# Local attention: scores of two heads in two 64-row halves of the TensorE array, and the value projection moved

## What is computed

```python
q, k, v = split(shift_token(x) @ wqkv, 3)        # 8 heads x 64
q = l2norm(q) * qs;  k = l2norm(k) * ksc
q, k = rotary_xpos(q, k)                         # a rotation by cos and sin tables
sim = einsum('bhwid,bhwjd->bhwij', bq, bk)       # 128 queries x (previous + own 128 keys)
attn = softmax(where(mask, -max, sim))
x = x + einsum('bhwij,bhwjd->bhwid', attn, bv) @ wo
```

## Time and profile before

| what | us |
|---|---|
| median of three runs (4228.1 to 4229.81) | 4228.54 |
| the profiled execution | 4233.28 |
| its span, first to last instruction | 4231.3 |
| one local attention, from its first to its last instruction (four in a launch) | about 287 |
| one window in its steady part | 17.00 |

### The profile page before, as it was taken

The page is one execution under the profiler, slowest core; times in us unless marked ns, Lnnn a source line. Parts: engine busy times, 40 slices in busy tenths (PEclk is TensorE's granted clock), DMA queues, the critical chain, the costliest instruction groups (busy, mean ns, idle before and its releaser), DMA issues. The chain is left out here.

```text
span 4231.3 us, 60343 instructions
## 1 busy us (share of the span) xinstructions
PE 3778.0 (89%) x19732; PEld 1808.6 (43%) x19732; DVE 2843.5 (67%) x7049; ACT 2050.9 (48%) x3685; POOL 919.6 (22%) x804
## 2 busy tenths in 40 slices
PE   7899977899988989898969999688999799899988
PEld 6233334233334555555542333342333355555555
DVE  3889856789856653565349897658897566436643
ACT  2366652266655651465123666423666466415641
POOL 1201013201014322332240010141010233223322
PEclk7799988799998999999987999897999899999999
DMA  3322002211010000000032220022220200100000
GB/s 77 48 31 32 1 3 42 41 23 27 14 42 22 6 26 31 22 6 6 20 71 31 31 32 1 2 50 33 31 32 2 61 8 1 52 20 13 1 11 25
DMA packets 129553, 108.89 MB, mean 26 GB/s; under 512 B 40872, under 2 KB 122320, under 8 KB 128208
## 3 DMA queue, kind: packets, MB, share of 16 engines
q1 hardware_dynamic: 129232, 104.92, 12.3%
HBM read 41.15 MB, written 4.19 MB: 11 GB/s over the span
## 5 line engine op out<-in xcount | busy, mean ns | idle before, releaser
L722 ACT ACTIVATE probs<-banks 128x1024 f32<-128x1024 f32 (+3 forms) x1280 | 1081.4, 895 | 756.1 <-PE banks L690 753.4
L761 DVE TENSOR_REDUCE chunk_max<-banks 128x1 f32<-128x512 f32 (+2 forms) x1728 | 1102.5, 684 | 73.3 <-PE banks L648 54.4
L648 PE MATMUL banks<-stack_k,stack_q 96*128 96x512 bf16 (+3 forms) x2560 | 825.2, 376 | 80.8 <-PEq L142 44.4
L690 PE MATMUL banks<-stack_q,stack_k 99*128 99x512 bf16 (+3 forms) x2560 | 662.0, 350 | 18.6 <-ACT probs L722 18.6
L667 PE MATMUL banks<-probs,values 128*17 128x512 f32 (+3 forms) x5120 | 591.9, 534 | 20.4 <-ACT probs L722 17.0
L648 PEld LDWEIGHTS banks<-stack_k,stack_q 96*128 96x128 bf16 x2560 | 241.4, 99 | 727.4 <-DVE chunk_max L761 402.4
L615 POOL TENSOR_SCALAR_AFFINE_SELECT probs<-probs 128x512 f32<-128x512 f32 x256 | 162.7, 636 | 1670.6 <-ACT probs L722 1667.4
L1321 ACT ACTIVATE probs_l<-probs_l,nmax 128x256 f32<-128x256 f32 x512 | 255.9, 500 | 342.2 <-DVE nmax L1444 340.7
L1198 PE MATMUL banks<-wqkv,hT 128*128 128x512 f32 x768 | 359.7, 606 | 2.6 <-issue 2.6
L690 PEld LDWEIGHTS banks<-stack_q,stack_k 99*128 99x128 bf16 x2560 | 232.5, 99 | 279.5 <-ACT probs L722 100.5
L1613 PE MATMUL banks<-hnT,w 128*128 128x512 f32 x704 | 315.4, 609 | 3.5 <-ACT hnT L1636 3.5
(11 more groups left out here) (189 smaller groups left out, 4933.5 us busy)
## 6 DMA issues: line engine op xcount, KB each, us to landing
stack_q<-parts SPq DMA_DIRECT2D x384, 64.0 KB, 2.4
stack_k<-parts SPq DMA_DIRECT2D x384, 64.0 KB, 2.4
xpos<-in_c_xpos SPq DMA_DIRECT2D x4, 2048.0 KB, 8.3
wqkv<-in_L_ffn_wqkv SPq DMA_DIRECT2D x12, 512.0 KB, 12.6
w<-in_L_ffn_w SPq DMA_DIRECT2D x16, 320.0 KB, 3.3
x_tok<-in_L_attn_x SPq DMA_DIRECT2D x8, 512.0 KB, 6.0
rope<-in_c_rope SPq DMA_DIRECT2D x2, 2048.0 KB, 7.5
hs_f<-x_mid SPq DMA_DIRECT2D x16, 256.0 KB
```

The source lines that it names most:

```text
L648: ins = pe.matmul(out, sq[0:KS, c, j0 + j, i * P:(i + 1) * P], sk[0:KS, cc, j0 + j, 0:width], start=True, stop=not (diag and heads > 1), s ...
L690: ins = pe.matmul(ps[:, SCORE + j, off:CH], keys, sq[0:KS + PARTS, c, j, off:CH], start=True, stop=True, skip_group_check=True)
L722: act.activation(probs[:, s % 2, 2 * half:2 * half + 2, off:CH], ps[:, SCORE + 2 * half:SCORE + 2 * half + 2, off:CH], ACT.Exp)\
L761: dve.tensor_reduce(chunk_max[:, n % 2, j:j + heads, i, cc], bank[:, 0:heads * width].rearrange("p (h n) -> p h n", h=heads), AX.X, ALU.ma ...
```

## The change

- The keys lose their block-diagonal form. `kT` holds both heads' keys in 128 partitions; ACT copies them in one instruction, not two, and POOL clears one slot instead of all.
- `scores` becomes two products for each pair: head 0 in rows 0 to 63 of the array, head 1 in rows 64 to 127, with 256 columns each, and each into a bank of its own. Three banks (3, 5, 6) go in turn over single heads: head i waits for the maximum of head i - 3. `maximum` waits and signals once for each head.
- v gives its bank to the scores and is projected into q's bank 1. It is projected in its own window, at p = 0 right behind the scores and ahead of `turn_h` and k; q moves to p = 1, since it has to wait until ACT has copied v out.
- ACT copies v at p = 0, squares k there behind it, and squares q at p = 1.
- DVE rotates q in one piece at p = 1, behind the scale.

```diff
-    BH, BQ, BK, BV, BO, BS, BT = 0, 1, 2, 3, 4, 5, 7
+    BH, BQ, BK, BO, BT = 0, 1, 2, 4, 7
+    BS = (3, 5, 6)
-    PROJECTED = ((1, 0), (), (2,), ())
...
-        kbd = sb("k_blocks", [P, NP, 2, SLOT, P])
+        kT = sb("kT", [P, NP, SLOT, P])
... project(w, i)
-                    bank, free, done = ((BQ, ("q_T_out", w), "qk_q"), (BK, ("k_T_out", 2 * w), "qk_k"),
-                                        (BV, ("v_out", w), "v_mm"))[i]
+                    bank, free, done = ((BQ, ("v_out", w), "qk_q"), (BK, ("k_T_out", w), "qk_k"),
+                                        (BQ, ("q_T_out", w + 1), "v_mm"))[i]
... scores(n)
-                    if n >= 2:
-                        pe.wait_ge(S["maxed"], n - 1)
-                    pe.matmul(ps[:, BS + n % 2, :].rearrange("p (a b n) -> p a b n", a=2, b=2), qT[:, p, :],
-                              kbd[:, p, :, s0:s1 + 1:s1 - s0, :], start=True, stop=True, skip_group_check=True)\
-                        .then_inc(S["scored"], 1)
+                    for h in range(2):
+                        i = 2 * n + h
+                        rows = slice(h * LD, (h + 1) * LD)
+                        if i >= 3:
+                            pe.wait_ge(S["maxed"], i - 2)
+                        pe.matmul(ps[:, BS[i % 3], 0:2 * P].rearrange("p (b n) -> p b n", b=2), qT[rows, p, :],
+                                  kT[rows, p, s0:s1 + 1:s1 - s0, :], start=True, stop=True, skip_group_check=True)\
+                            .then_inc(S["scored"], 1)
... PE, pair n
                         scores(n)
+                        if p == 0:
+                            project(w, 2)
                         if p == 0 and w + 2 < NT:
                             turn_h(w + 2)
-                        if w + 1 < NT:
-                            for i in PROJECTED[p]:
-                                project(w + 1, i)
+                        if p < 2 and w + 1 < NT:
+                            project(w + 1, 1 - p)
... ACT, qk_out and pair n
-                    for h in range(2):
-                        rows = slice(h * LD, (h + 1) * LD)
-                        act.copy(kbd[rows, :, h, w % SLOT, :], ps[rows, BK, :].rearrange("p (n m) -> p n m", n=NP))\
-                            .then_inc(S["k_T_out"], 1)
+                    act.copy(kT[:, :, w % SLOT, :], ps[:, BK, :].rearrange("p (n m) -> p n m", n=NP)).then_inc(S["k_T_out"], 1)
-                        if w + 1 < NT:
-                            for i in PROJECTED[p]:
-                                if i < 2:
-                                    square(w + 1, i)
-                                else:
-                                    v_take(w + 1)
+                        if p == 0:
+                            v_take(w)
+                        if p < 2 and w + 1 < NT:
+                            square(w + 1, 1 - p)
... DVE, maximum(n) and pair n
-                    dve.wait_ge(S["scored"], n + 1)
                     dve.wait_ge(S["p_T"], n + 1)
                     for h in range(2):
-                        ins = dve.tensor_tensor_reduce(...)
-                    ins.then_inc(S["maxed"], 1)
+                        dve.wait_ge(S["scored"], 2 * n + h + 1)
+                        dve.tensor_tensor_reduce(..., in0=ps[:, BS[(2 * n + h) % 3], 0:2 * P], ...).then_inc(S["maxed"], 1)
-                    if p == 1 and ahead:
-                        rotate(w + 1, 0, (0,))
                     if p == 2 and ahead:
                         squares(w + 1, 0)
                     scale(n)
                     if p == 0 and ahead:
                         squares(w + 1, 1)
                         rotate(w + 1, 1)
                     if p == 1 and ahead:
-                        rotate(w + 1, 0, (1,))
+                        rotate(w + 1, 0)
                         normalise(w + 1)
```

More of the change, by code:

```diff
@@ L1213, in scores @@
                         pe.wait_ge(S["q_T_out"], w + 1)
-                        pe.wait_ge(S["k_T_out"], 2 * (w + 1))
-                    if n >= 2:
-                        pe.wait_ge(S["maxed"], n - 1)
+                        pe.wait_ge(S["k_T_out"], w + 1)
                     s0, s1 = order(w)
-                    pe.matmul(ps[:, BS + n % 2, :].rearrange("p (a b n) -> p a b n", a=2, b=2), qT[:, p, :],
-                              kbd[:, p, :, s0:s1 + 1:s1 - s0, :], start=True, stop=True, skip_group_check=True)\
-                        .then_inc(S["scored"], 1)
+                    for h in range(2):
[6 more added lines that the diff above has]
+                            .then_inc(S["scored"], 1)
                 def turn_p(n):
@@ L1257, in _ @@
                 turn_h(0)
-                for i, come in ((1, "w_k"), (0, "w_q"), (2, "w_v")):
+                for i, come in ((1, "w_k"), (0, "w_q")):
                     pe.wait_ge(early[come], 16)
@@ L1267, in _ @@
                         scores(n)
+                        if n == 0:
+                            pe.wait_ge(early["w_v"], 16)
+                        if p == 0:
+                            project(w, 2)
                         if p == 0 and w + 2 < NT:
                             turn_h(w + 2)
-                        if w + 1 < NT:
-                            for i in PROJECTED[p]:
-                                project(w + 1, i)
+                        if p < 2 and w + 1 < NT:
+                            project(w + 1, 1 - p)
                         if p == 3:
@@ L1304, in v_take @@
                     act.wait_ge(S["v_mm"], w + 1)
-                    act.copy(v[:, w % SLOT, :], ps[:, BV, :]).then_inc(S["v_out"], 1)
+                    act.copy(v[:, w % SLOT, :], ps[:, BQ, :]).then_inc(S["v_out"], 1)
                 def qk_out(w):
@@ L1310, in qk_out @@
                     act.wait_ge(S["k_T"], w + 1)
-                    if w == 0:
-                        act.wait_ge(S["zero_k"], 2)
-                    for h in range(2):
-                        rows = slice(h * LD, (h + 1) * LD)
-                        act.copy(kbd[rows, :, h, w % SLOT, :], ps[rows, BK, :].rearrange("p (n m) -> p n m", n=NP))\
-                            .then_inc(S["k_T_out"], 1)
+                    act.copy(kT[:, :, w % SLOT, :], ps[:, BK, :].rearrange("p (n m) -> p n m", n=NP)).then_inc(S["k_T_out"], 1)
                 def exp(n):
-                    act.wait_ge(S["maxed"], n + 1)
+                    act.wait_ge(S["maxed"], 2 * (n + 1))
                     for h in range(2):
@@ L1335, in _ @@
                 square(0, 0)
-                v_take(0)
                 h_out(1)
@@ L1362, in _ @@
                 pool.memset(mhalf[:, :], -0.5).then_inc(S["halves"], 1)
-                pool.memset(kbd[:, :, :, :, :], 0.0).then_inc(S["zero_k"], 1)
+                pool.memset(kT[:, :, SLOT - 1, :], 0.0).then_inc(S["zero_k"], 1)
                 pool.memset(v[:, SLOT - 1, :], 0.0).then_inc(S["zero_k"], 1)
@@ L1383, in _ @@
                     if w >= 2:
-                        pool.wait_ge(S["maxed"], NP * (w - 1))
+                        pool.wait_ge(S["maxed"], 2 * NP * (w - 1))
                     pool.tensor_tensor(inv_q[:, w % 2, :], ssum[:, q], mhalf[:, q], ALU.pow).then_inc(S["inv_n"], 1)
@@ L1440, in maximum @@
                     m = later[:, 0 if w == 0 else 1 if w % SLOT == 0 else 2, :]
-                    dve.wait_ge(S["scored"], n + 1)
                     dve.wait_ge(S["p_T"], n + 1)
                     for h in range(2):
-                        ins = dve.tensor_tensor_reduce(out=pr[:, n % 2, h, :], in0=ps[:, BS + n % 2, h * 2 * P:(h + 1) * 2 * P],
-                                                       in1=m, scale=inv_q[:, w % 2, 2 * p + h:2 * p + h + 1], scalar=3e38, op0=ALU.add, op1=ALU.min,
-                                                       accum_out=nmax[:, n % 2, h:h + 1])
-                    ins.then_inc(S["maxed"], 1)
+                        dve.wait_ge(S["scored"], 2 * n + h + 1)
+                        dve.tensor_tensor_reduce(out=pr[:, n % 2, h, :], in0=ps[:, BS[(2 * n + h) % 3], 0:2 * P], in1=m,
+                                                 scale=inv_q[:, w % 2, 2 * p + h:2 * p + h + 1], scalar=3e38,
+                                                 op0=ALU.add, op1=ALU.min, accum_out=nmax[:, n % 2, h:h + 1])\
+                            .then_inc(S["maxed"], 1)
                 def scale(n):
```

## The result

The changed kernel took 4245.97 us (median of 6 runs, 4244.49 to 4246.84) against 4229.80 for the kernel before (6 runs, 4228.1 to 4232.31): a ratio of 1.0037, with a 95% interval of 1.0025 to 1.0049. The forecast was 4238 in a range of 4219 to 4265: the sign and the range hold, but the loss is 16 us where 9.5 was forecast.

A forecast was written before the change was run, and what follows sets the result against it. PE was taken to bound the kernel, its saving turning into waits behind k. Edges and steady windows gave 2.2 us a stage, 2.4 with semaphores, four times +9.5 on the 4228.54 median: 4238 us, range 4219 to 4265.

The forecast's parts named there:

- What bounds the kernel: Steady local-attention window before the change: PE sets the pace, 16.32 us of work plus a 0.68 gap at `turn_h`, 17.00.
- A block of scores: PE's scores for one pair: the two row halves overlap, so 0.63 us plus the next work's first load, for 0.96.
- Rival 1: Score products on PE: the two halves don't overlap at all, 0.43 us more per block on the path, 4265 us; chance 0.10.
- rival 2: Score products on PE: the halves overlap in part, three slots, 0.216 us more per block, 4252 us; chance 0.08.
- What is late next: Steady window after the change: k behind v delays DVE, POOL and `turn_qk`; 16.99 us, PE's saving turned into waits.
- every sign of the list: Timeline signs of a right forecast: window 16.9 to 17.1, paired products starting together, named PE and DVE waits, smaller `turn_h` gap.
- Rival 3: Steady window: PE still sets the pace if k's last product ends at 3.5 or earlier; 15.3 us, 4140 in all; chance 0.16.
- The edges: Windows outside the steady part, shorter than 17.0 before: with steady windows 2.2 us a stage, 2.4 with extra semaphores.
- Start and window 0: Each stage's start up to window 1's first scores: these come at 1312.2 for 1311.66, +0.5 us.
- window 1: Second window of each stage, 16.26 us before with no gap and no `add` yet: +0.7 us.
- Window 14: Second-last window of each stage, 16.07 us before without `turn_h`: 16.77 after, +0.7 us.
- window 15: Last window of each stage: gets v's projection, but DVE's turns of 2.78 us set its pace; +0.1 us.

The follow-up runs named there:

- the last row of the table: Kernel before with `turn_h` behind the projections and `normalise` in the third pair's exp: 4193.9 us, window 16.29; with two score halves added, 4132.48 us, window 15.29.
- the run with k first: Changed kernel with k projected ahead of v and `turn_h`, and squared on ACT ahead of copying v: 4175.7 us, ratio 0.9876.
- the schedule alone: Kernel before with the moved projections, squares, v copy and q rotation, but its block-diagonal keys, 512-column scores and two score banks: 4259.17 us, ratio 1.007.
- the run with a busy start: Changed kernel with head 1's product for the third pair of window 0 issued six times instead of once: 4237.56 us, ratio 1.002.

## Why the prediction was right in sign and short in size

- **What bounds the kernel: right.** PE set the pace in 16.32 of work and a gap; the last row of the table shows the 16.3, and the gap went with the order.
- **A block of scores: right.** 0.63 measured and forecast. Rival 1 would show a block 0.43 longer and rival 2 one 0.22 longer; both are ruled out by the rows above. Rival 2 was what the strict order of starts in the Trainium skill (TensorE: Matmul & The Clock Gate, "What overlaps and what doesn't") would give; the trace here disagrees, since heads whose two rows each follow one another in the program take two slots together.
- **What is late next: right, leg by leg.** 16.98 for 16.99, and every sign of the list was seen: `turn_p` waiting for ACT, DVE idle ahead of k's sums and nowhere ahead of the second maximum, the gap at `turn_h` gone. That k's place behind v is the cause is shown by the run with k first. That head 1's wait is not is shown by that run, which keeps the wait and has a window of 16.04, together with the schedule alone, which has no such wait and a window of 17.20.
- **Rival 3, PE still sets the pace: not in this order,** but its condition was the right one: k's last product ending 3.5 or earlier after the window's start. With k first it ends near 2.6 and DVE waits for scores once more; yet the window is 16.04 and not the 15.3 of PE's work, so the condition brings most of the gain and not all of it: the rest waits at p = 3.
- **The edges: the step that failed.** "Start and window 0" was +0.5 a stage and "window 1" +0.7; measured are +2.8 (from -0.9 and +12.2 over four stages) and +1.3. The walk kept PE at the upper clock once it was granted, though it had PE wait for ACT at p = 2. In window 0 the `turn_p` and `pv` of the window before, which fill PE's time at p = 0 and 1, are missing, so that wait is 1.88 and not 0.63. After it the clock fell, for 3.4 to 6.8 us in each stage. The run with a busy start shows this to be the cause of 6.3 us, of the 11.5 by which the two pieces were forecast too short; window 1 then takes 16.97, as walked. Once the clock is out of the way, a second step shows: the wait of `turn_p` for the scale, 0.57, that is 2.3 over four stages, for which the walk had put nothing behind `turn_qk`. Some 3 us stay open; no run settles them. In the run with a busy start (4 there, since its starts are longer) they lie almost wholly in the second and fourth stage, for which the walk took over the figures of the first: there the lower clock reaches 4.7 us into window 0, and 2.8 to 2.9 in the kernel before. Window 14 (+2.7 for +2.8) was right and window 15 (+0.9 for +0.4) close.
- **What the total owes to chance.** The local attentions alone lost 18.8 us by the traces, twice the 9.5 forecast. The spans, 13.4 apart, come nearer to the forecast only through the code outside, which is the same and differed by 5.4 between the two profiled executions; the forecast had no term for that, and no run settles what moves it. The medians are 16.2 apart.

## What to carry to other kernels

Work cut from the busiest engine is gained only if its instructions still come in an order in which the next engine's chain starts as early as before: walk one steady window with every engine in program order, and ask of each moved product who waits for it. Look at the first windows by themselves, since work that fills a wait in the steady part is missing there, and if the clock falls behind such a wait, that costs about as much again (0.9 to 2.2 us in a stage here, behind a wait of 1.88). And try the parts apart: here the part that gained (61 us) was hidden by the part that rearranged, and two order edits gave another 36.

## What the runs showed of the hardware

Two 64-row halves of the array ran the fp32 products of two heads at the same time, each with its own bank: the block of four rows took 0.63 us to the next start, and two slots of 0.216 are 0.43 of that. The other 0.20 is put down, as an estimate, to 0.10 for the first load and 0.10 for the change of shape behind the block. The granted clock fell to 0.50 behind a wait of 1.88 us in window 0 of all four stages, and five repeated products in that wait kept it at 1.00: extra work made the first two windows shorter, by 6.3 us over the four stages. Behind a wait of 1.98 in the schedule alone it fell in two stages of four.
